# Convolution stage of a decoder: the output bias as one three-part bf16 product, and the rows of x brought in by transposing products

## What is computed

```python
xc = silu(pointwise(causal_depthwise_conv(x)) + pw_b)
x1 = x + xc
logits = x1 @ router_w.T + router_b              # 8 experts, the best 2 are kept
rw = one_hot(top_i) * softmax(top_v)             # summed over the two
ye = silu(einsum('bsd,eod->bseo', x1, expert_w) + expert_b)
combined = einsum('bse,bseo->bso', rw, ye)
moe_out = combined @ out_w.T + out_b
h = rmsnorm(x1 + moe_out, norm_w)
ff = gelu(h @ ff_down_w.T + ff_down_b) @ ff_up_w.T + ff_up_b
x = layernorm(x + h + ff)
```

## Time and profile before

| | us |
|---|---|
| median of 3 timed runs | 3676.05 (3666.92 to 3680.37) |
| span of the profiled execution | 3676.0 |
| PE busy in it | 2923.5 (80%) |
| DVE busy | 2180.6 (59%) |
| ACT busy | 1827.8 (50%) |
| POOL busy | 1827.1 (50%) |
| convolution stage alone, first product to last z | about 2560 to 2907 |

### The profile page before, as it was taken

How to read it: one execution, slowest core, us unless ns; L and a number is a source line. 1 busy time by engine, 2 the same in 40 slices (tenths; PEclk the granted TensorE clock), 3 DMA queues, 4 the chain that set the end, 5 groups by cost and what they waited for, 6 DMA issues and landing times. The chain is left out here.

```text
span 3676.0 us, 83888 instructions
## 1 busy us (share of the span) xinstructions
PE 2923.5 (80%) x28814; PEld 2031.9 (55%) x28814; DVE 2180.6 (59%) x5986; ACT 1827.8 (50%) x3516; POOL 1827.1 (50%) x1735
## 2 busy tenths in 40 slices
PE   2778867897888699954529997996999869995884
PEld 2667755574555456642416664664445536664774
DVE  2111134657888578862347886777898677884125
ACT  0333334744555466621216665775466677662442
POOL 3542354535777655526465554664033655553425
PEclk9999988899999799975559998998999889996997
DMA  8566652020101121114621112221000012222764
GB/s 289 181 186 187 187 150 76 22 5 25 41 37 43 44 75 68 65 47 129 167 52 43 57 54 88 87 86 54 1 1 1 1 30 63 72 64 91 213 209 143
DMA packets 325161, 315.46 MB, mean 86 GB/s; under 512 B 111348, under 2 KB 244886, under 8 KB 324505
## 3 DMA queue, kind: packets, MB, share of 16 engines
q1 hardware_dynamic: 283240, 261.98, 23.5%
q0 software_dynamic: 16384, 33.59, 3.0%
q10 hardware_dynamic: 25264, 16.40, 1.5%
HBM read 167.28 MB, written 60.69 MB: 62 GB/s over the span
## 5 line engine op out<-in xcount | busy, mean ns | idle before, releaser
L936 DVE TENSOR_TENSOR moe_first_tile_y<-moe_first_out_ps,moe_first_expert_w 128x256 f32<-128x256 f32 x85 | 35.7, 423 | 372.5 <-PE moe_first_out_ps L1067 180.3
L1056 PE MATMUL moe_first_hid_ps<-moe_first_tile_xT,moe_first_expert_w 128*128 128x256 f32 x680 | 182.5, 415 | 42.3 <-ACT moe_first_hid L1118 39.9
L1067 PE MATMUL moe_first_out_ps<-moe_first_expert_w,moe_first_hid 128*128 128x128 f32 x1360 | 173.6, 281 | 11.4 <-issue 10.3
L1067 PEld LDWEIGHTS moe_first_out_ps<-moe_first_expert_w,moe_first_hid 128*128 128x128 f32 x1360 | 172.5, 197 | 17.2 <-issue 11.6
L1137 POOL DMA_INDIRECT slot_x<-x_tok,moe_first_slots x128 | 123.9, 968 | 110.1 <-DVE moe_first_slots L908 48.6
L1118 ACT ACTIVATE moe_first_hid<-moe_first_hid_ps,moe_first_expert_w 128x256 f32<-128x256 f32 x340 | 138.2, 473 | 68.8 <-PE moe_first_hid_ps L1056 43.2
L794 POOL DMA_INDIRECT moe_first_token_y<-slot_y,moe_first_slots x128 | 123.8, 967 | 95.8 <-issue 67.7
L1056 PEld LDWEIGHTS moe_first_hid_ps<-moe_first_tile_xT,moe_first_expert_w 128*128 128x128 f32 x680 | 135.0, 210 | 65.2 <-issue 45.0
L1870 POOL TENSOR_TENSOR causal_k_blocks<-causal_k_T,headmask 128x1024 f32<-128x1024 f32 x64 | 121.3, 1898 | 99.6 <-PE causal_scores L1480 94.0
L1870 POOL TENSOR_TENSOR alibi_k_blocks<-alibi_k_T,headmask 128x1024 f32<-128x1024 f32 x64 | 121.3, 1896 | 94.1 <-PE alibi_scores L1480 90.0
L1870 POOL TENSOR_TENSOR full_k_blocks<-full_k_T,headmask 128x1024 f32<-128x1024 f32 x64 | 120.7, 1896 | 84.2 <-PE full_scores L1480 79.2
(11 more groups left out here) (561 smaller groups left out, 9047.8 us busy)
## 6 DMA issues: line engine op xcount, KB each, us to landing
moe_first_expert_w<-in_L_attn_experts SPq DMA_DIRECT2D x85, 578.0 KB
moe_last_expert_w<-in_L_ffn_experts SPq DMA_DIRECT2D x53, 578.0 KB
moe_first_tile_x<-slot_x SPq DMA_DIRECT2D x85, 128.0 KB
slot_y<-moe_first_tile_y SPq DMA_DIRECT2D x85, 128.0 KB
slot_x<-blank ACTq DMA_DIRECT2D x2, 4992.0 KB
L_ffn_tile_x<-slot_x SPq DMA_DIRECT2D x32, 256.0 KB
slot_y<-L_ffn_tile_y SPq DMA_DIRECT2D x32, 256.0 KB
moe_last_tile_x<-slot_x SPq DMA_DIRECT2D x53, 128.0 KB
```

Source lines behind the costliest of these rows:

```text
L936: dve.tensor_tensor(y_out[:, q, :, :], out_bank[q][:, 0:SLOT_TILE].rearrange("p (s d) -> p s d", s=SPAN), over(wall[:, j % RING, 2 * FF + ...
L1056: last = pe.matmul(hid_bank[h][:, SLOT_TILE * (b % 2):SLOT_TILE * (b % 2) + SLOT_TILE], wall[:, j % RING, 128 * b:128 * b + 128], xT[:, j ...
L1067: last = pe.matmul(out_bank[j % 2][:, D * s:D * s + D], hid[:, j % 2, b, TILE * s:TILE * s + TILE], wall[:, j % RING, FF + D * b:FF + D * ...
```

## The change

The bias of z is loaded to three partitions behind the expert biases, in one tile of 1024 + 128 columns, and the split into three bf16 parts now runs over 1152 columns. In the z block the four fp32 products of x_T with the identity become four transposing products (one pass each), the four fp32 bias products become one bf16 product over all 512 columns, and the four fp32 products with out_w come last.

```diff
-    expert_b = sub.load([3, E * D], op("expert_b").rearrange("(o e) d -> o (e d)", o=1)
-                        .to_broadcast([3, E * D]))
+    BW = E * D + D
+    biases = sub.weight([3, BW])
+    sub.loads.append((biases[:, 0:E * D], op("expert_b").rearrange("(o e) d -> o (e d)", o=1).to_broadcast([3, E * D])))
+    sub.loads.append((biases[:, E * D:BW], op("out_b").rearrange("(o d) -> o d", o=1).to_broadcast([3, D])))
     out_s = sub.load([128, D], op("out_wT"))
-    out_b = sub.load([1, D], op("out_b").rearrange("(o d) -> o d", o=1))
...
-        high, middle = sb("expert_b_high", [3, E * D], BF16), sb("expert_b_middle", [3, E * D], BF16)
-        rest, low = sb("expert_b_rest", [3, E * D]), sb("expert_b_low", [3, E * D])
-        parts_b, ones_b = sb("expert_b_parts", [3, E * D], BF16), sb("ones_bf", [3, 128], BF16)
+        high, middle = sb("bias_high", [3, BW], BF16), sb("bias_middle", [3, BW], BF16)
+        rest, low = sb("bias_rest", [3, BW]), sb("bias_low", [3, BW])
+        parts_b, ones_b = sb("bias_parts", [3, BW], BF16), sb("ones_bf", [3, 128], BF16)
...
-                dve.tensor_copy(high[:, :], expert_b[:, :]).then_inc(split_steps, 1)
+                dve.tensor_copy(high[:, :], biases[:, :]).then_inc(split_steps, 1)
...
                 for k in range(PER):
-                    t, z = PER * c + k, z_bank[:, D * k:D * k + D]
-                    pe.matmul(z, net.x_T[:, TILE * t:TILE * t + TILE], net.ident[:, :], start=True, stop=False)
-                    pe.matmul(z, combined_T[:, c % 2, TILE * k:TILE * k + TILE], out_s[:, :], start=False, stop=False)
-                    last = pe.matmul(z, net.ones[0:1, :], out_b[:, :], start=False, stop=True)
+                    t = PER * c + k
+                    pe.matmul(z_bank[:, D * k:D * k + D], net.x_T[:, TILE * t:TILE * t + TILE], net.ident[:, :],
+                              start=(k == 0), stop=False, is_transpose=True)
+                pe.matmul(z_bank[:, :], ones_b[:, :], over(parts_b[:, E * D:BW], PER), start=False, stop=False)
+                for k in range(PER):
+                    z = z_bank[:, D * k:D * k + D]
+                    last = pe.matmul(z, combined_T[:, c % 2, TILE * k:TILE * k + TILE], out_s[:, :], start=False,
+                                     stop=(k == PER - 1))
                 last.then_inc(z_ready, 1)
```

More of the change, by code:

```diff
@@ L3104, in split_bias @@
             def split_bias():
-                dve.tensor_copy(high[:, :], expert_b[:, :]).then_inc(split_steps, 1)
+                dve.tensor_copy(high[:, :], biases[:, :]).then_inc(split_steps, 1)
                 dve.wait_ge(split_steps, 1)
-                dve.tensor_tensor(rest[:, :], expert_b[:, :], high[:, :], ALU.subtract).then_inc(split_steps, 1)
+                dve.tensor_tensor(rest[:, :], biases[:, :], high[:, :], ALU.subtract).then_inc(split_steps, 1)
                 dve.wait_ge(split_steps, 2)
```

## The result

Both kernels were run six times on one chip: 3675.14 us median before (3666.92 to 3680.37), 3657.18 after (3647.36 to 3666.59). The ratio is 0.9954 [0.9942, 0.9967], 18 us less, against a forecast of 3656 and a range of 3641 to 3671. The time lies on the line between faster by 0.5% and no change, as the forecast did.

A forecast was written before the change was run, and what follows sets the result against it. In settled steps PE (20.00 us) and a DVE-POOL ring (19.98) both bound the convolution stage, PE alone afterwards. Gains 3.0 + 0.4 + 5.4 + 5.1 + 1.5 + 3.5 + 2.2, less 0.8, make 20.3: 3676.0 to 3656, range 3641 to 3671.

The forecast's parts named there:

- three stretches: Convolution stage: DVE waits for PE before step 6, PE and the ring tie in 6 to 11, PE alone afterwards.
- The z block: Each chunk's z products on PE: from 4.12 us to 1.93, taken as 2.2 less, bounds 1.7 and 2.4.
- Item 1: Steps up to 5: DVE's waits of 2.2 and 0.8 us go away, the ring runs 3.0 us ahead.
- item 7: Stage's start: splitting the bias over 1152 columns, no longer 1024, costs 0.8 us, bounds 0.4 to 2.5.
- the ring: Settled steps 6 to 11: DVE and POOL hold each other in a 19.98 us cycle that faster PE doesn't move.
- Item 2: Steps 6 to 11: the ring keeps 19.98; L3027 may get in before L3314; 0.4 us in all, bounds 0 and 1.2.
- Item 3: Turn of step 12: DVE's lead over PE, 5.4 us, is set free; sum so far 8.8.
- Item 4: Steps 12 to 14: PE sets the pace, 6.6 us saved less 1.5 once for ACT, so 5.1; sum 13.9.
- Items 5 and 6: Step 15 saves 1.5 us at most, capped by POOL; step 16 saves 3.5, step 17 2.2; sum 21.1.
- Rival 1: Whole stage: PE is the bound everywhere and each saving counts, 37 us less, 3639; 12 in 100.
- Rival 2: Steps 12 to 16: ACT or DVE late in each, so the end gives less; 10 us in all, 3666; 26 in 100.
- Rival 3: Steps 6 to 14: PE's idle time brings half clock, slower, 3696 at 12 us a step; 7 in 100.

The follow-up runs named there:

- E9: Changed kernel with the bias as four three-part bf16 products of 128 columns, each behind its tile's output product; ratio to the kernel before 0.9960.
- E5: Changed kernel with the output bias's 128 columns split only in chunk 1's turn of mix_two; ratio to the kernel before 0.9957.
- E3: Kernel before, with POOL's three residual operations held until the first part of combine is done; ratio to the kernel before 1.0002.
- E4: Changed kernel, with POOL's three residual operations held until the first part of combine is done; ratio to the kernel before 0.9953.
- E7: Changed kernel with one POOL operation of three, up bias and norm weight of the residual left out (different result); 3653.4 us, timed once.
- E2: Kernel before with only the transposing products for x's rows, bias still four fp32 products; ratio to the kernel before 1.0044.
- E10: E2 with its fp32 bias as one product over the bank's 512 columns; ratio to the kernel before 0.9937.
- E1: Changed kernel with x's rows brought in by plain fp32 identity products, bias one bf16 product; ratio to the kernel before 0.9942.
- E6: E5 with x's rows brought in by plain fp32 identity products instead of transposes; ratio to the kernel before 0.9961.

## Why the prediction was right

The total was right, and so was the division into three stretches that carries it. In part the total was luck: two errors at the start offset each other. By its steps:

- *The z block*: 1.93 forecast, 1.84 measured; the lower bound of 2.4 for the saving was the nearer one (2.39 a step where PE is the bound).
- *Item 1 and item 7.* L3067 of chunk 7, the first settled one, is at 133.8 before, 132.1 after, 129.9 with the late split. So the ring ran 3.9 us ahead (3.0 forecast), and 2.2 of it were lost at the start (0.8 forecast). The split itself is priced rightly: with the wide split and an early rise of the clock E9 has the same L3067 at 130.7, 0.8 behind E5. The other 1.4 go with the clock's rise, at 28.0 us in this trace and 25.3 in E9; item 7 names such a thing only in its bounds, 0.4 to 2.5. The two errors, 0.9 and 1.4, cancelled for the most part, by luck.
- *Item 2.* The ring holds: 19.74, within the 19.5 to 20.0 in which I said it would be the bound. L3028 gets in first, as forecast. From chunk 7 to chunk 12 this gave 1.2 us (99.9 and 98.7), 0.4 forecast, 1.2 its upper bound.
- *Item 3.* turn_combined of step 12: 8.5 us earlier (252.2 and 243.7). Forecast 8.8 less 0.8.
- *Item 4.* Steps 13, 14, 15: 9.8, 12.2 and 13.9 earlier; forecast 13.1 net. The first gain is small and the following ones full, which is what "once, 1.5 us" meant.
- *Items 5 and 6.* Step 16's turn_combined is 15.2 earlier (14.6 net), the last z_sq 19.5 (348.3 and 328.8; 20.3 net forecast). But at the mark only 17.7 is left. The step that failed is the last sentence of the sum, that the stages behind simply start when this one ends: from the first to the third product of the next stage (L2470) 14.2 us pass, where 12.9 did (338.2 to 352.4, and 357.2 to 370.1). 1.3 of the lost 1.8 are there. No run was made for it, but the two traces show where it goes: 0.8 in the second group of products, since the clock rises near its start before (2917.9) and near its end after (2902.8), and 0.5 where DVE's L2526 falls beside an operation of POOL (L2561, from 2910.78) and holds up the residual behind it. Before, then after:

```profile
2917.42 2.11 PE L2470 MATMUL L_ffn_experts<-L_attn_xn_T,weights_even 128*128 128x512 f32 x4
...
2926.76 0.17 DVE L2526 TENSOR_SCALAR L_attn_ss_max<-L_attn_ss 128x4 f32<-128x4 f32 x1
```

```profile
2900.72 2.96 PE L2470 MATMUL L_ffn_experts<-L_attn_xn_T,weights_even 128*128 128x512 f32 x4
...
2910.91 0.94 DVE L2526 TENSOR_SCALAR L_attn_ss_max<-L_attn_ss 128x4 f32<-128x4 f32 x1
```

- *Rival 1*, that the ring loosens, was wrong for the change, and E3 and E4 show why: the held time moves with POOL's work. Cut that work, and the rival's world comes about (E7).
- *Rival 2*, that the end gives less, hardly came: from turn_combined of step 12 to the last z_sq the gain grew by 11.0 us, where the forecast had 12.3 and the rival 2.2. With the 1.8 above it is 9.2 at the mark.
- *Rival 3*, the clock. PE does idle some 2 us a step, and the clock stays at 1.00; the mechanism I priced, idle time, did not come. The other one, in the sentence on the Trainium skill ("TensorE: Matmul & The Clock Gate", "Part 4: PE-mode transpose"), came in E2: with PE never idle, the clock fell behind the transposes. By that rule alone E9, E10 and the change should suffer too, and they don't. I gave the slower side 0.06 for the change; its transposing half alone is slower (1.0044), if by less than the half per cent that counts as slower.

What the prediction did not say is who earns the gain. It priced the two halves as one, and by the runs it is the bias product and the order of the block; the transposes add nothing that the times show (E1, and E6 beside E5).

## What to carry to other kernels

Where two engines are full, give each its own period before pricing a saving, and price it by stretches: here 2.3 us a step on PE were worth 0.24 in the settled stretch and paid mainly behind it, once DVE had less to do. In these kernels GpSimd's operations on values in SBUF cost a full VectorE some three quarters of their length (2.9 for 3.8 us), and moving them to another place didn't help; a bias that GpSimd adds may be cheaper as one three-row bf16 product on the matrix engine. Put small products of one kind in an unbroken row and add a bias once over the whole bank, before thinking of a cheaper type. And before a loss of a microsecond or two is put down to an edit, compare another trace that shares the edit: the place where the clock rises or falls moved by as much between kernels here.

## Hardware behaviour I had not expected

- The granted clock fell to 1.2 GHz with PE busy in every window, behind 8 transposing products and 3.2 us of narrow ones, half of them with one row of weights, at seven of the first twelve z blocks (E2). In E9 and E10, with the same transposes and 2.2 and 2.1 us of products behind them, it didn't; which difference matters stays open.
- The pair of records of a 128-column fp32 product takes 0.25 us in a row of eight, 0.42 between products of another kind (E9, E10).
- POOL's elementwise operations of 1.1 to 1.4 us hold DVE 0.8 to 1.1 us each, even when DVE is in a run of short scalar_tensor_tensor operations: 8.19 us become 11.12 under three of them (E4).
- The clock's rise to 2.4 GHz at the stage's start lies between 21.6 and 28.0 us after the first convolution in the fourteen traces, also where the same edit stands there (25.3 in E9, 28.0 in the change), and moves step 0's product by 1.2 us and more. The mean granted clock over 80 us at the end of the stage lies between 0.72 and 0.87.
